# The first pass over the adjacency is multiplied inside the build, stage by stage

## The reference

```python
edge_index = jnp.stack([src, dst])
x = _layernorm(x + _L0_gnn_ref(x, edge_index, ...), axis=-1)
x = _layernorm(x + _L1_gnn_ref(x, src, dst, edge_attr_16, ...), axis=-1)

# L0, two of these with a relu between (64 -> 128 -> 64)
agg = segment_sum(x[src], dst); cnt = segment_sum(1, dst)
h = agg / max(cnt, 1) @ W_l.T + b_l + x @ W_r.T

# L1, three of these, a batch norm and relu behind the first two;
# every node has a loop edge whose attributes are ones
m = concat([x[dst], x[src], edge_attr], 1) @ W.T + b
h = relu(segment_sum(m, dst))
```

## Time and profile before

| | us |
|---|---|
| median of 3 runs | 1293.20 (1293.18 to 1293.88) |
| profiled execution, its own time | 1293.01 |
| its span in the profile | 1291.2 |
| build, up to | 429.4 |
| pass 0 with the matmuls ahead for pass 1 | 429.4 to 624.4 |
| passes 1 to 4 and the normalisations | 624.4 to 1291.2 |
| mean granted TensorE clock, share of 2.4 GHz | 0.891 |

### The profile page before, as it was taken

One profiled execution on the slowest core, in us unless ns is written; L12 is line 12 of the kernel. 1 busy time (PEld: TensorE's weight loads), 2 busy tenths in 40 slices (PEclk: granted clock), 3 DMA queues, 4 the chain that ended last, 5 costly groups with the idle time before them and its releaser, 6 DMA issues. The chain is left out here.

```text
span 1291.2 us, 20445 instructions
## 1 busy us (share of the span) xinstructions
PE 1117.8 (87%) x8160; PEld 667.1 (52%) x8160; DVE 728.6 (56%) x1452; ACT 341.6 (26%) x626; POOL 89.4 (7%) x102
## 2 busy tenths in 40 slices
PE   0358878998689879999999999999789998899994
PEld 0358878897688534445455554444334444334442
DVE  6799999999998302121244356654455655324344
ACT  2444565566666100000000001011231012300000
POOL 4111211211111000000000000000000000000001
PEclk9966767877557889999999999999889999989997
DMA  6223343556565897575357760765503765107660
GB/s 157 59 65 115 118 152 116 196 177 202 181 226 199 333 344 243 231 265 202 117 195 282 289 233 13 285 243 225 200 13 124 299 244 226 75 21 293 247 239 19
DMA packets 69304, 240.84 MB, mean 187 GB/s; under 512 B 31760, under 2 KB 44811, under 8 KB 53747
## 3 DMA queue, kind: packets, MB, share of 16 engines
q1 hardware_dynamic: 62276, 191.48, 41.6%
q0 software_dynamic: 6928, 48.00, 9.9%
HBM read 197.66 MB, written 41.79 MB: 185 GB/s over the span
## 5 line engine op out<-in xcount | busy, mean ns | idle before, releaser
L1141 PE MATMUL PM<-Aring,Xop 128*128 128x512 fp8e4 (+1 forms) x2450 | 498.1, 363 | 0.0
L1141 PEld LDWEIGHTS PM<-Aring,Xop 128*128 128x128 f16 x2450 | 227.3, 98 | 266.8 <-issue 16.3
L637 PE MATMUL PW<-key,lo 128*128 128x52 fp8e4 (+2 forms) x2466 | 200.2, 258 | 10.2 <-ACT F L698 10.2
L637 PEld LDWEIGHTS PW<-key,lo 128*128 128x128 fp8e4 x2466 | 189.6, 122 | 18.3 <-ACT F L698 11.2
L1141 PE MATMUL PM<-Ares,Xop 128*128 128x512 fp8e4 x735 | 171.5, 389 | 9.3 <-DMA Ares<-adj 7.1
L1596 ACT ACTIVATE F<-PH,bag 64x512 f32<-64x512 f32 (+1 forms) x39 | 25.4, 657 | 382.3 <-PE PH L1324 382.2
L1434 DVE TENSOR_TENSOR S<-PM,rc 128x256 f32<-128x256 f32 (+1 forms) x50 | 18.7, 414 | 190.0 <-PE PM L1141 149.1
L1141 PEld LDWEIGHTS PM<-Ares,Xop 128*128 128x128 f16 x735 | 70.7, 100 | 100.2 <-issue 13.1
L652 PE MATMUL PA<-Ares,ea 128*128 128x32 f16 x1867 | 112.1, 234 | 0.1
L652 PEld LDWEIGHTS PA<-Ares,ea 128*128 128x128 f16 x1867 | 109.1, 118 | 0.2 <-issue 0.2
L1436 DVE TENSOR_SCALAR S<-PM 128x256 f32<-128x256 f32 (+1 forms) x75 | 31.4, 418 | 130.4 <-PE PM L1141 118.5
(11 more groups left out here) (136 smaller groups left out, 950.5 us busy)
## 6 DMA issues: line engine op xcount, KB each, us to landing
Aring<-adj SPq DMA_DIRECT2D x90, 1568.0 KB, 9.8
adj<-Xop POOLq DMA_DIRECT2D x12, 1568.0 KB, 5.8
adj<-stage POOLq DMA_DIRECT2D x12, 1568.0 KB, 6.2
Ares<-adj SPq DMA_DIRECT2D x6, 1568.0 KB, 15.8
rc<-rc_d SPq DMA_DIRECT2D x24, 256.0 KB, 9.9
rc<-ea_sum SPq DMA_DIRECT2D x36, 128.0 KB, 5.7
Aring<-adj SPq DMA_DIRECT2D x5, 784.0 KB, 4.4
eaf<-in_erow SPq DMA_DIRECT2D x62, 51.0 KB
```

Of the source, the lines that this page charges most:

```text
L637: last = nc.tensor.matmul(PW[bank % RING][:, c:c + 52 * (z - y)].rearrange("p (u b) -> p u b", b=2), lo[:, h % 2, i, :].bitcast(f8), key[: ...
L1141: last = nc.tensor.matmul(o, x[:, h, :], rhs, start=h == 0, stop=h == NT - 1)
```

## The change

Within the build, as soon as stage st is taken apart, TensorE multiplies it by `Xop[0]` into a PSUM bank of its own, `PX` (`product`, 49 matmuls of 256 columns); ScalarE copies the raw sums to one of two buffers `raw` (`take`), and GpSimd issues their store to a new DRAM tensor `s0` (`keep_product`). The product of a stage stands on TensorE at the head of the step after the one in which it is taken apart, behind the transposes and in front of L637. The bank is taken from the ring `PW`, which has four now. To make room in SBUF, gathered rows have three buffers in place of four and the converted tables two in place of three. `unpack` waits in addition for the product two stages back, which read the same stage buffer.

Pass 0 does no `main` any more. Its sums come from `s0` in four loads (GROUPS) into what is `Aring[0]` later, the reciprocal counts in two broadcast loads (blocks 0 to 5, then the others) into what is `Aring[1]` later. VectorE multiplies the two straight from SBUF. The late counts are done behind the sums of block 1. The adjacency of blocks 0 to 2 is loaded to `Ares` only in pass 0, behind all of these, and the ring's first two blocks when the last sums of pass 0 are scaled. The matmuls ahead wait for `Ares` block 0.

```diff
-RING = 5
+RING = 4
+GROUPS = [(0, 4), (4, 8), (8, 11), (11, NB)]
+HALFWAY = 6
...
+            "s0": nc.dram_tensor("s0", [128, NP], f32, kind="Internal").ap(),
...
-        rows = within(0, [128, 4, 128, 2], i32)
+        rows = within(0, [128, 3, 128, 2], i32)
-        vs = within(0, [128, 3, 2, 128], i16)
+        vs = within(0, [128, 2, 2, 128], i16)
+        raw = within(0, [128, 2, SW], f32)
+        PX = ps("PX", [128, 512])
...
-            for b in range(RB - 1):
-                if b == 0:
-                    sp.wait_ge(s_sm, TS)
-                    sp.wait_ge(s_lo, NCH)
-                else:
-                    sp.wait_ge(s_oh, NH)
-                for h in range(2):
-                    sp.wait_ge(s_st[h], 16 * (b + 1))
-                    sp.dma_start(m["Ares"][:, b, h, :], m["adj"][2 * b + h]).then_inc(m["s_res"][b], 16)
...
+            def keep_product(st):
+                n = stage_width(st)
+                g.wait_ge(s_raw, st + 1)
+                g.dma_start(m["s0"][:, st * SW:st * SW + n], raw[:, st % 2, 0:n]).then_inc(s_so[st % 2], 16)
...
                 for st in unpacked_after(h) if h <= NH else []:
                     keep(st)
+                for st in unpacked_after(h - 1) if h >= 1 else []:
+                    keep_product(st)
...
                 if st >= 2:
                     v.wait_ge(s_st[st % 2], 16 * (st // 2))
+                    v.wait_ge(s_px, st - 1)
...
+            def product(st):
+                n = stage_width(st)
+                pe.wait_ge(s_un, st + 1)
+                if st >= 1:
+                    pe.wait_ge(s_raw, st)
+                of = stage[st % 2][:, 0:NT * n // 2].bitcast(f8).rearrange("p (h d) -> p h d", h=NT)
+                for h in range(NT):
+                    last = nc.tensor.matmul(PX[:, 0:n], m["Xop"][0][:, h, :], of[:, h, :], start=h == 0, stop=h == NT - 1)
+                last.then_inc(s_px, 1)
...
                     turn(h // 2 + 3)
+                for st in unpacked_after(h - 1) if h else []:
+                    product(st)
                 pe.wait_ge(s_oh, h + 1)
...
+            for h in (NH - 1, NH):
+                for st in unpacked_after(h):
+                    product(st)
...
+            def take(st):
+                n = stage_width(st)
+                act.wait_ge(s_px, st + 1)
+                if st >= 2:
+                    act.wait_ge(s_so[st % 2], 16 * (st // 2))
+                nc.scalar.copy(raw[:, st % 2, 0:n], PX[:, 0:n]).then_inc(s_raw, 1)
...
                     for st in sums_after(h - 1):
                         sums(st)
+                    for st in unpacked_after(h - 1):
+                        take(st)
+            for st in unpacked_after(NH):
+                take(st)
...
+        if fused:
+            sp.wait_ge(m["s_cd"], 16)
+            reciprocals(0)
+            products(0)
+            sp.dma_start(F[0:64, :], ins["xT"]).then_inc(t["s_xt"], 16)
+            for i in range(2):
+                sp.wait_ge(m["s_eo"][i], 16 * (13 - i))
+            there, here = spread(m, "ea_sum", t["cnt"], EARLY, NP)
+            sp.dma_start(here, there).then_inc(t["s_cl"], 16)
+            products(1)
+            late_factors()
+            sp.wait_ge(m["s_st"][1], 16 * 12)
+            reciprocals(1)
+            for i in range(2, len(GROUPS)):
+                products(i)
+            sp.dma_start(F[64:97, 0:NP], m["ea_sum"][:, 0:NP]).then_inc(t["s_ea"], 16)
+            for b in range(RB):
+                for h in range(2):
+                    sp.dma_start(t["Ares"][:, b, h, :], m["adj"][2 * b + h]).then_inc(m["s_res"][b], 16)
+            sp.wait_ge(s_r, NB)
+            for b in range(2):
+                for h in range(2):
+                    sp.dma_start(t["Aring"][:, b, h, :],
+                                 m["adj"][2 * (RB + b) + h]).then_inc(t["s_ar"][b][h], 16)
+            return
...
-            if (0 if p == 0 else 1 if p < 3 else 2) <= i < NB and not slow:
+            if p >= 1 and (1 if p < 3 else 2) <= i < NB and not slow:
                 main(i)
...
-                pe.wait_ge(s_S, NB)
+                if p == 1:
+                    pe.wait_ge(s_S, NB)
+                else:
+                    landed(pe, 0)
                 ahead(0, 20)
...
-                    of = by_quad(PM[b % 2][:, h:h + w])
+                    of = by_quad(sraw[:, c + h:c + h + w] if fused else PM[b % 2][:, h:h + w])
                     if p <= 1:
-                        last = nc.vector.tensor_tensor(part, of, natural(rc[:, b % 2, h:h + w]), ALU.mult)
+                        by = rcall[:, c + h:c + h + w] if fused else rc[:, b % 2, h:h + w]
+                        last = nc.vector.tensor_tensor(part, of, natural(by), ALU.mult)
...
+            if fused and i == 2:
+                late_counts()
```

More of the change, by code:

```diff
@@ L182, in gnn @@
             "s_eo": [sem(f"s_eo{i}") for i in range(2)],
+            "s_so": [sem(f"s_so{i}") for i in range(2)],
             "s_res": [sem(f"s_res{i}") for i in range(RB)],
@@ L278, in build @@
         s_sti = sem("s_sti")
-        s_rows = [sem(f"s_rows{i}") for i in range(4)]
+        s_rows = [sem(f"s_rows{i}") for i in range(3)]
         s_nat = sem("s_nat")
@@ L787, in layers @@
             "csum": m["csum"],
+            "s_sr": [sem(f"s_sr{i}") for i in range(len(GROUPS))],
+            "s_rb": [sem(f"s_rb{i}") for i in range(2)],
             "fl": sb("fl", [1, 16]),
@@ L1107, in _ @@
     def _(sp):
-        if not slow:
-            for i in range(2):
-                sp.wait_ge(m["s_eo"][i], 16 * (13 - i))
-        there, here = spread(m, "ea_sum", t["cnt"], 0 if slow else EARLY, NP)
-        sp.dma_start(here, there).then_inc(t["s_cl"], 16)
         if slow:
+            there, here = spread(m, "ea_sum", t["cnt"], 0, NP)
+            sp.dma_start(here, there).then_inc(t["s_cl"], 16)
             sp.dma_start(m["F"][0:64, :], ins["xT"]).then_inc(t["s_xt"], 16)
@@ L1171, in propagate @@
     s_told = sem("told")
-    mm0 = NB * p
+    mm0 = NB * (p - 1)
+    fused = p == 0 and not slow
+    sraw, rcall = (t["Aring"][:, i].rearrange("p s c -> p (s c)").bitcast(f32) for i in range(2))
     nk = [0]
@@ L1198, in late_factors, with products, reciprocals @@
             sp.wait_ge(t["s_cd"], 16)
+        def products(i):
+            b0, b1 = GROUPS[i]
+            c0, c1 = b0 * 512, min(NP, b1 * 512)
+            for z in range(2):
+                sp.wait_ge(m["s_so"][z], 16 * len(range(z, min(NST, 2 * b1), 2)))
+            sp.dma_start(sraw[:, c0:c1], m["s0"][:, c0:c1]).then_inc(t["s_sr"][i], 16)
+        def reciprocals(i):
+            c0, c1 = ((0, HALFWAY * 512), (HALFWAY * 512, NP))[i]
+            src = m["rc_d"][c0:c1].rearrange("(o n) -> o n", o=1)
+            sp.dma_start(rcall[:, c0:c1], src.broadcast_to([128, c1 - c0])).then_inc(t["s_rb"][i], 16)
@@ L1200, in _ @@
         if p == 0:
-            if slow:
-                late_factors()
-            else:
-                sp.wait_ge(m["s_cd"], 16)
+            late_factors()
         factors(0)
         factors(1)
-        if p == 0 and not slow:
-            sp.dma_start(F[0:64, :], ins["xT"]).then_inc(t["s_xt"], 16)
-            for h in range(2):
-                sp.dma_start(t["Ares"][:, 2, h, :], m["adj"][4 + h]).then_inc(m["s_res"][2], 16)
-            for b in range(2):
-                for h in range(2):
-                    if b == 1 and h == 0:
-                        sp.wait_ge(m["s_st"][1], 16 * 12)
-                    sp.dma_start(t["Aring"][:, b, h, :],
-                                 m["adj"][2 * (RB + b) + h]).then_inc(t["s_ar"][b][h], 16)
-            late_factors()
-            sp.dma_start(F[64:97, 0:NP], m["ea_sum"][:, 0:NP]).then_inc(t["s_ea"], 16)
@@ L1277, in landed @@
         if b < NB - 1:
-            lag = sum(1 for z in range(p) if ((NB - RB) * z + NB - 1 - RB) % 2 == i)
+            lag = sum(1 for z in range(p - 1) if ((NB - RB) * z + NB - 1 - RB) % 2 == i)
             engine.wait_ge(t["s_ar"][i][1], 16 * (k - lag))
@@ L1420, in sums @@
             else:
-                v.wait_ge(t["s_mm"], mm0 + b + 1)
+                if fused:
+                    v.wait_ge(t["s_sr"][next(i for i, (_, e) in enumerate(GROUPS) if b < e)], 16)
+                    v.wait_ge(t["s_rb"][0 if b < HALFWAY else 1], 16)
+                else:
+                    v.wait_ge(t["s_mm"], mm0 + b + 1)
                 if b >= 2:
                     v.wait_ge(s_g if p == 1 else s_h, b - 1)
-            v.wait_ge(s_c[b % 2], 16 * (b // 2 + 1))
+            if not fused:
+                v.wait_ge(s_c[b % 2], 16 * (b // 2 + 1))
             to = S[:, b % 2, 0:n]
```

37 lines of the change are left out of this document (21 added, 16 removed).

## The result

| | before | after |
|---|---|---|
| median, same chip | 1293.54 | 1324.65 (1323.01 to 1326.33, 4 runs) |
| ratio, 95% interval | | 1.0238 [1.0218, 1.0258] |
| span in the profile | 1291.2 | 1324.4 |
| build, up to | 429.4 | 584.8 |
| build's end to pass 1 | 195.0 | 70.6 |

Slower by 31.1 us in the medians, 33.2 in the profiled spans; 38.1 was forecast. The build grew by 155.4 us and pass 0 shrank by 124.4.

What follows compares the result with a forecast made beforehand. TensorE and VectorE were taken as nearly full in the build, TensorE alone in the first pass. Terms 169.2 - 7.1 + 6 - 130 = +38.1 on 1293.0 gave 1331 us, range 1315 to 1347.

Steps and rivals of the forecast that it cites:

- Products: Build: 25 products add 169.2 us to TensorE, 7.0 each behind attribute sums with 3.3 us of low clock.
- Gaps filled: Build, before the transposes of even steps: products fill only 7.1 of 33.2 us of TensorE's gaps; bounds 0 and 33.
- The chain behind take: Build: from product end through ScalarE's copy, conversions, tables and spreads to the next transpose, about 13.2 us.
- Stalls inside the keys: Build, six evacuation stalls in the key matmuls: four PSUM buffers and take ahead of evacuations add 6 us; bounds 0 and 25.
- Build's end: Build: ends at 597.5 us, from 429.4 + 169.2 - 7.1 + 6.
- Pass 0: From the build's end to pass 1: 65 us where it was 195; bounds 58 and 80.
- all the covers: First pass: late factors, adjacency block 0 and ring loads all arrive before needed; if not, block 6 costs up to 10 us.
- VectorE loses nothing: Build: VectorE needs some 11.8 us a step against TensorE's 17 to 20, and its new wait in unpack costs nothing.
- Small pools: Build: three row buffers for four and two tables for three wait on work a whole step old, costing nothing.
- A: Build: products lift the clock (5.4 us for 7.0, -34) and fill half the remaining gaps (-13): 1284 us; chance 0.10.
- B: Build: ScalarE behind take holds evacuation and tables more, new TensorE gaps in 20 steps, +25: 1356 us; chance 0.22.
- C: Build: low clock for whole products, +91: 1422 us; chance 0.03.

Runs made afterwards that it cites:

- e8: Changed kernel with only the first loads of pass 0 cut smaller (1.9 MB ahead of the first dense products, not 4.2): 1315.23 us.
- e3: Changed kernel with each product behind the keys' matmuls and ahead of the attribute sums, take and store one step later: 1305.04 us.
- e4: Changed kernel with products where they are, but take of a step's last stage and its store one step later, behind the evacuations: 1316.18 us.
- e2: Changed kernel with the product ahead of the transposes in even steps, not behind them: 1308.56 us.
- e7: Kernel before the change with only its smaller buffers (four PSUM banks, three of rows, two of tables): 1294.15 us, ratio 1.000.
- e6: e5 with the first loads of pass 0 cut smaller: 1278.40 us, ratio 0.987 to the kernel before.
- e5: Changed kernel with products behind the keys' matmuls up to step 26, at the step's head from 27, take and store following: 1277.52 us.
- e11: e5 run once more, the same kernel: 1278.51 us, ratio 0.988 to the kernel before.

## Why the prediction was right, step by step

The side and the mechanism were right: 25 products on TensorE's path at 5.4 to 7.9 us (the last 2.9) cost more than pass 0 gave back. That the sum came within 5 us (33.2 for 38.1 in the spans) is partly luck: the build came out 12.7 us shorter than forecast, pass 0 and what follows 7.8 us longer, and the same build in e8 ended 8.3 us earlier still. Term by term:

- **Products, 169.2 forecast, 171.5 measured** (169.3 of bursts and 2.2 in four waits for take). In the timeline 20 of the 21 single ones are 6.5 to 7.9 us, the three chained ones 5.5, the last 2.9. The hit is partly luck. One single found the full clock (5.5 us), others were at 1.2 GHz for 4 us and more, not the 3.3 that I took, and the handover to take was 0.55, not 0.8. e3 shows that the place is the cause: without attribute sums in front the same matmuls took 27 us less. What in the burst brings the clock down, its 32 columns or something else about it, no run tried.
- **Gaps filled, 7.1 forecast, 12.5 measured.** The sum of gaps before the transposes was to be 26.1 and is 20.7. The chain behind take was right in kind, as e4 shows, which halves the wait by moving take alone; its length was overestimated. What I did not weigh is that the product's place behind the transposes was itself the loss: e2 takes 12.7 of the 20.7 away. The two overlap and can't be added.
- **Stalls inside the keys, +6 forecast, -3.3 measured** (6.9 for 10.2). This step failed most, by 9.3 us and with the wrong sign. e7 gives +2.0 for the smaller ring alone; behind a product ScalarE has had time to catch up, so the stalls it starts a step with are shorter (1.5 us at most, 3.4 before). That last reason is read from the waits and was not tried by itself.
- **Build's end, 597.5 forecast, 584.8 measured**: 429.4 + 171.5 - 12.5 - 3.3 = 585.1.
- **Pass 0, 65 forecast, 70.6 measured.** The blocks' 3.0 us, the matmuls ahead and all the covers held: no gap on TensorE from 602.3 to 655. The start was mis-sized, 17.5 us for 13. TensorE's first dense matmul, and the loads that SP issues up to xT, with their time to landing (issues: count, KB, median us; the second line also holds the group issued behind xT):

```profile
602.32 2.05 PE L1367 MATMUL PH<-S,wl 128*128 128x512 f32 x2 [17.04 <-DMA F<-in_xT]
```

```profile
Aring<-rc_d SPq DMA_DIRECT2D x1, 1536.0 KB, 6.6
Aring<-s SPq DMA_DIRECT2D x2, 1024.0 KB, 13.3
F<-in_xT SPq DMA_DIRECT2D x1, 1568.0 KB, 16.5
```

  I had taken xT's 11.4 us of the earlier trace rows for a transfer that now stands third, behind 2.6 MB. e6 and e8 confirm it: with half as much up to xT the wait fell to 9.8 us.
- **VectorE loses nothing**: right, 284 us busy of 454, and none of TensorE's waits names it. But the sign I named, VectorE waiting for TensorE before its large one-hots, was wrong: 2.4 us. It waits for ScalarE's conversions behind take instead, and 52.1 us in unpack for the product two stages back, as these waits of VectorE in the build show. That second wait was costed at nothing and did cost nothing here; in e3, with the product later in the step, it led to the stall of 11.4 us.

```profile
DVE ea L559 <- ACT eax L712: 103.0, 18, 8.7
DVE Xop L543 <- PE PX L629: 33.3, 3, 15.6
DVE stage L543 <- PE PX L629: 18.8, 2, 12.5
DVE lo L523 <- PE PW L657: 2.4, 2, 2.1
```

- **Small pools**: nothing in the kernel before, shown by e7; beside the products they were not tried by themselves. From pass 1 on 2.2 us more than before; no run explains that, and it is within what two profiles of one kernel differ by there (666.3 us in e5, 668.7 in e11).

Of the rivals, A was wrong for this kernel, but its price was there to take by another placing: in e5 the bursts are 28 us shorter than in the kernel after and the gaps before the transposes 19 us, together A's 34 + 13, and a stage cost 4.4 us, under the 5.3 from which A decides. B named an engine that matters, since moving take alone (e4) was worth 8.5 us, a third of B's price; but its new gaps did not come, as TensorE waits for ScalarE 29.8 us in this build and waited 43.4 before. C did not happen.

## What to carry to other kernels

Moving matmuls into a stretch where TensorE has idle time pays only by the idle time that they really cover and at the clock that they really find: work out both per unit, and compare with what the unit cost where it was. Then try the unit's place within the step before judging the change: the places of the product and of its copy together were worth 47 us here, the difference between 2.4% slower and 1.2% faster. Behind a wait that has nothing to do with it, or directly behind the matmuls after which the clock is low, the unit was dear; behind matmuls that lost nothing by the low clock it was cheap. One place need not serve all steps: where two units fall in one step, the release of a buffer counted for more than the clock. And profile one kernel twice before reading a few microseconds into a difference: the same build ended 8.3 us apart (after and e8).

## What the runs showed of the hardware

- A TensorE without gaps ran at 1.2 GHz: bursts of 64 matmuls of 32 columns (3.8 us) were followed by a granted clock of 0.50, at 160.9 us for 4 us of 256-column matmuls. Of the 21 products that stand behind such a burst 20 took 6.5 to 7.9 us, and the one at 221.43 us took 5.5. The 256-column matmuls took 0.110 us apiece at full clock (5.4 per 49).
- One kernel's clock falls differently in each execution. e11's executions range from 1285.8 us at a mean granted clock of 0.906 to 1275.4 at 0.916; e5's, the same kernel, from 1277.2 to 1282.7. The kernel before ranges over 5.5 and 6.6 us in the runs beside them.
- 1.6 MB into 64 partitions (xT) landed 16.5 us after its issue behind 2.6 MB; from 594 to 603 us the DMAs moved 167 to 255 GB/s, and 402 to 444 GB/s from about 625 us on, when blocks of adjacency for 128 partitions were loaded. Other loads were issued with xT, so these rates don't show that the 64 partitions are the reason.
